# A float32 product split into high and low parts: other engines write the parts of its first instance, and its last chunk goes tile by tile

## The reference

```python
# x: 8 x 1024 x 512, cond: 8 x 512; D = 512
ae = layernorm(cond, ln_g, ln_b)
h = gelu(ae @ w1 + b1)                       # exact gelu
x_a, x_b = split(h @ w2 + b2)                # each 8 x 512 x 8 (rank 8)
layer = base_layer + einsum('bdr,bkr->bdk', x_a, x_b)
x = x + (x + einsum('btc,bco->bto', x, layer))          # first layer
ys = cond / sqrt(D)
d = rsqrt(einsum('bi,io->bo', ys*ys, weight*weight) + 1e-8)
x = x + einsum('bsi,io->bso', x * ys[:, None, :], weight) * d[:, None, :]
```

## Time and profile before

| what | value |
| --- | --- |
| median of 3 runs | 293.89 us (293.83 to 294.56) |
| profiled execution: its own time, and its span | 293.79 us, 292.1 us |
| PE busy | 287.6 us (98%) |
| PEld busy | 226.5 us (78%) |
| DVE busy | 198.8 us (68%) |
| ACT busy | 153.5 us (53%) |
| POOL busy | 18.1 us (6%) |
| mean granted TensorE clock | 0.998 of full speed |

### The profile page before, as it was taken

The page is one execution under the profiler, slowest core; times in us unless marked ns, Lnnn a source line. Parts: engine busy times, 40 slices in busy tenths (PEclk is TensorE's granted clock), DMA queues, the critical chain, the costliest instruction groups (busy, mean ns, idle before and its releaser), DMA issues.

```text
span 292.1 us, 3792 instructions
## 1 busy us (share of the span) xinstructions
PE 287.6 (98%) x1400; PEld 226.5 (78%) x1400; DVE 198.8 (68%) x309; ACT 153.5 (53%) x233; POOL 18.1 (6%) x35
## 2 busy tenths in 40 slices
PE   8999999999999999999999999999999999999995
PEld 8775566657688888888888888888888888888884
DVE  4889342237577899994699988766783749762672
ACT  4763141306373548774548765634781645443951
POOL 5000000000131202000202000020000000000000
PEclk9999999999999999999999999999999999999999
DMA  6998899987042311589512589201132493101205
GB/s 189 368 426 300 324 406 384 362 311 281 2 120 89 153 72 72 166 263 378 203 72 109 181 266 417 109 0 72 72 139 79 147 362 142 72 0 74 106 38 215
DMA packets 13409, 55.05 MB, mean 188 GB/s; under 512 B 1616, under 2 KB 1616, under 8 KB 11088
## 3 DMA queue, kind: packets, MB, share of 16 engines
q1 hardware_dynamic: 10368, 44.07, 41.1%
q10 hardware_dynamic: 3024, 10.75, 9.3%
HBM read 38.03 MB, written 16.78 MB: 188 GB/s over the span
## 4 chain that ended last, share of the span: by engine, by line
PE 97%; DVE 1%; issue 0%; ACT 0%; POOL 0%; ACTq 0%; POOLq 0%
PE tile L1143 30%; PE tile L1174 26%; PE tile L992 12%; PE aux L1028 6%; PE acc L960 5%; PE tile L1109 4%; PE tile L975 3%; PE spare L1028 3%; PE acc L1028 3%; PE tile L931 2%; PE aux L1014 1%; PE aux L938 1%; PE aux L1082 1%; PE spare L1014 1%; PE acc L1014 1%; DVE rs L664 0%
## 5 line engine op out<-in xcount | busy, mean ns | idle before, releaser
L1143 PE MATMUL tile<-xs,qs 128*128 128x512 f32 x384 | 90.3, 389 | 0.0
L1143 PEld LDWEIGHTS tile<-xs,qs 128*128 128x128 f32 x384 | 72.1, 188 | 15.0
L1174 PE MATMUL tile<-xs,qs 128*128 128x512 f32 x336 | 77.5, 389 | 0.0
L1174 PEld LDWEIGHTS tile<-xs,qs 128*128 128x128 f32 x336 | 63.1, 188 | 13.1
L767 DVE TENSOR_TENSOR xs<-stream,xs 128x1024 fp32r<-128x1024 f32 x30 | 36.2, 1219 | 12.6 <-ACT xs L428 12.4
L483 ACT ACTIVATE stream<-tile,dts 128x512 f32<-128x512 f32 x32 | 21.8, 688 | 36.4 <-PE tile L1143 36.4
L372 ACT CAST rs<-rtmp 128x512 fp32r<-128x512 f32 x32 | 19.9, 621 | 37.2 <-PE tile L992 24.2
L664 DVE TENSOR_TENSOR rs<-rtmp,rs 128x512 fp32r<-128x512 f32 x32 | 22.0, 688 | 25.6 <-ACT rs L372 25.2
L992 PE MATMUL tile<-rs,w0s 128*128 128x512 f32 x144 | 34.7, 395 | 0.1
L992 PEld LDWEIGHTS tile<-rs,w0s 128*128 128x128 f32 x144 | 26.5, 188 | 10.0 <-issue 4.2
L428 ACT CAST xs<-stream 128x1024 fp32r<-128x1024 f32 x30 | 31.1, 1048 | 3.7 <-ACT stream L483 2.3
(11 more groups left out here) (139 smaller groups left out, 247.7 us busy)
## 6 DMA issues: line engine op xcount, KB each, us to landing
stream<-in_w2u SPq DMA_DIRECT2D x13, 1024.0 KB, 8.7
stream<-in_xT SPq DMA_DIRECT2D x20, 512.0 KB, 5.9
out<-stream ACTq DMA_DIRECT2D x20, 512.0 KB, 2.6
xr<-in_xT SPq DMA_DIRECT2D x12, 512.0 KB, 5.0
out<-stream SPq DMA_DIRECT2D x11, 512.0 KB, 3.0
xr<-in_w2u SPq DMA_DIRECT2D x3, 1024.0 KB, 7.7
w1s<-in_w1n SPq DMA_DIRECT2D x4, 256.0 KB, 5.1
base<-in_wm SPq DMA_DIRECT2D x1, 1024.0 KB, 8.1
```

The source lines that it names most:

```text
L1143: last = nc.tensor.matmul(tiles[o][:], q_slot(b, cc)[:, u, cols], x_slot(b, (h, cc // 2))[:, v, cc % 2], start=cc == 0 and (u, v) == (0, 0 ...
L1174: last = nc.tensor.matmul(tiles[bank + m][:], q_slot(b, q)[:, u, cols], x_slot(b, x)[:, v, k], start=opens and k == 0 and (u, v) == (0, 0) ...
```

## The change

- DVE writes the high part of chunks 0 and 1 of R_0 itself: `r_direct` is the scaling pass with its output in `rs` (fp32r). The pass into `rtmp` is still made, a little later, since the low part needs it. ACT's two casts r_high(0, 0) and r_high(0, 1) go.
- POOL adds the 2s: it builds a matrix `ident2` with 2 on the diagonal (a memset and an affine_select, before the other constants), and adds it to each of the four diagonal blocks as they land. DVE's four add_two go. These four adds stand ahead of the sixteen casts for perm.
- The last chunk of the first product goes tile by tile, three matmuls for each tile, and starts once both low parts are there. The transposition for the hidden layer follows tile 1.
- The small steps of the layernorm come later in DVE's list, behind both parts of chunk 1. In the norms' chain w0_low(3) moves behind the first step, and r_low(0, 3) behind the last.
- On ACT the cast w0_high(1) moves ahead of w1_square(1).

```diff
+            nc.gpsimd.memset(ident2, 2.0).then_inc(pool_step, 1)
+            pool.wait_ge(pool_step, 5)
...
+            nc.gpsimd.affine_select(out=ident2, in_=ident2, compare_op=ALU.is_equal, fill=0.0, base=0,
+                                    pattern=[[-1, P]], channel_multiplier=1).then_inc(twos_ready, 1)
...
+            pool.wait_ge(twos_ready, 1)
+            for kc in range(KC):
+                pool.wait_ge(w0_loaded[kc], 16)
+                blk = w0raw[:, kc, kc * P:(kc + 1) * P]
+                nc.gpsimd.tensor_tensor(blk, ident2, blk, ALU.add).then_inc(w0_eyed, 1)
...
             w0_high(0)
-            r_high(0, 0)
             w1_square(0)
...
+            w0_high(1)
             w1_square(1)
-            w0_high(1)
-            r_high(0, 1)
...
+            def r_direct(kc):
+
+                nc.vector.tensor_scalar(rs[:, kc, 0], w1s[:, kc], ys[:, ORDER[0], kc:kc + 1], None,
+                                        ALU.mult).then_inc(r_hi, 1)
...
-            add_two(0)
             dve.wait_ge(w1_loaded[0], 16)
-            r_scale(0, 0)
+            r_direct(0)
             dve.wait_ge(sum_done, 3)
             step(nc.vector.tensor_scalar(row(2, B), aux[0][:, 64:64 + B], 1.0 / D, LN_EPS, ALU.mult, ALU.add))
             w0_low(0)
+            r_scale(0, 0)
             r_low(0, 0)
-            add_two(1)
             dve.wait_ge(w1_loaded[1], 16)
+            r_direct(1)
+            w0_low(1)
             r_scale(0, 1)
+            r_low(0, 1)
...
+                kc = KC - 1
+                pe.wait_ge(w0_lo, KC)
+                pe.wait_ge(r_lo, KC)
+                for cc in range(KC):
+                    for u, v in ((0, 0), (0, 1), (1, 0)):
+                        last = nc.tensor.matmul(tiles[cc][:], w0s[:, u, kc, cc * P:(cc + 1) * P], rs[:, kc, v],
+                                                start=False, stop=(u, v) == (1, 0))
+                    last.then_inc(tile_done, 1)
+                    if cc == 1:
+                        between(kc, 1, 0)
```

More of the change, by code:

```diff
@@ L91, in cond_residual_kernel @@
         w0nat = base[:, 4]
+        ident2 = base[:, 0, 0, 0:P]
         asp, csp = qs[:, 4, 0], qs[:, 4, 1]
@@ L121, in cond_residual_kernel @@
         mask_ready = sem("mask_ready")
+        twos_ready = sem("twos_ready")
+        first_scaled = sem("first_scaled")
         ys_ready = sem("ys_ready")
@@ L327, in _ @@
             nc.gpsimd.memset(eye4[:], 0.0).then_inc(pool_step, 1)
-            pool.wait_ge(pool_step, 4)
+            nc.gpsimd.memset(ident2, 2.0).then_inc(pool_step, 1)
+            pool.wait_ge(pool_step, 5)
             nc.gpsimd.affine_select(out=ident[:], in_=ones[:], compare_op=ALU.is_equal, fill=0.0, base=0,
                                     pattern=[[-1, P]], channel_multiplier=1).then_inc(consts_ready, 1)
+            nc.gpsimd.affine_select(out=ident2, in_=ident2, compare_op=ALU.is_equal, fill=0.0, base=0,
+                                    pattern=[[-1, P]], channel_multiplier=1).then_inc(twos_ready, 1)
             nc.gpsimd.affine_select(out=sel3, in_=sel3, compare_op=ALU.not_equal, fill=1.0, base=0,
@@ L369, in r_high @@
             def r_high(b, kc):
-                act.wait_ge(r_eyed, b * KC + kc + 1)
+                act.wait_ge(r_eyed, b * KC + kc - 1)
                 rs_free(act, b, kc)
@@ L635, in _ @@
                                     mybir.AxisListType.X, ALU.add).then_inc(sum_done, 1)
[L637 to L640, removed]
             def w0_low(kc):
@@ L653, in r_scale @@
                 if b == 0:
-                    scaled.then_inc(r_eyed, 1)
+                    scaled.then_inc(r_eyed if kc > 1 else first_scaled, 1)
                     return
@@ L660, in r_scale @@
                                                ALU.add).then_inc(r_eyed, 1)
+            def r_direct(kc):
+                nc.vector.tensor_scalar(rs[:, kc, 0], w1s[:, kc], ys[:, ORDER[0], kc:kc + 1], None,
+                                        ALU.mult).then_inc(r_hi, 1)
             def r_low(b, kc):
                 dve.wait_ge(r_hi, b * KC + kc + 1)
+                if b * KC + kc < 2:
+                    dve.wait_ge(first_scaled, kc + 1)
                 nc.vector.tensor_tensor(rs[:, kc, 1], rtmp[:, kc % RTMP], rs[:, kc, 0].bitcast(F32),
@@ L675, in r_build @@
                 r_low(b, 3)
-            dve.wait_ge(consts_ready, 1)
-            add_two(0)
             dve.wait_ge(w1_loaded[0], 16)
-            r_scale(0, 0)
+            r_direct(0)
             dve.wait_ge(sum_done, 3)
@@ L692, in _ @@
             step(nc.vector.scalar_tensor_tensor(row(0, B), row(7, B), 1.5, row(5, B), ALU.add, ALU.mult))
-            w0_low(1)
-            r_low(0, 1)
-            add_two(2)
             dve.wait_ge(w1_loaded[2], 16)
@@ L703, in _ @@
             r_low(0, 2)
-            add_two(3)
             dve.wait_ge(w1_loaded[3], 16)
             r_scale(0, 3)
-            w0_low(3)
-            r_low(0, 3)
             dve.wait_ge(d2_turned, 1)
             d_next(nc.vector.tensor_scalar(by_chunk(3), turned(1), D_EPS, None, ALU.add))
+            w0_low(3)
             dve.wait_ge(d_root, 1)
@@ L718, in _ @@
                                            dts[:].rearrange("p b k -> p k b"), by_chunk(3), ALU.mult))
+            r_low(0, 3)
             r_scale(1, 0)
@@ L964, in first_base @@
             def first_base(between):
-                for kc in range(KC):
+                for kc in range(KC - 1):
                     for u, v in ((0, 0), (1, 0), (0, 1)):
@@ L975, in first_base @@
                             last = nc.tensor.matmul(tiles[cc][:], w0s[:, u, kc, cc * P:(cc + 1) * P], rs[:, kc, v],
[L976 to L980, removed]
+                                                    start=kc == 0 and (u, v) == (0, 0), stop=False)
+                        if v:
                             last.then_inc(r_used, 1)
                         between(kc, u, v)
+                kc = KC - 1
[8 more added lines that the diff above has]
+                        between(kc, 1, 0)
             def base_tiles(b, between):
```

## The result

The changed kernel takes 295.06 us (median of 11 executions, 294.53 to 295.58), and the kernel before 293.89 us in as many beside it. The ratio is 1.0033, with a 95% interval from 1.0023 to 1.0044. That is 0.3% slower, and 0.4 us above the upper end of the forecast range (293.3 to 294.7).

The account below looks back on a forecast made before the run. PE was taken to bound the kernel (97% of the chain that ended last), with 0.50 us of gaps here. 293.79 - 0.05 + 0.1 = 293.84, the median 0.10 above that execution: forecast 293.9 us, range 293.3 to 294.7.

Parts of the forecast that it names:

- DVE then starts w0_low(2) no later than before: Ahead of chunk 2: the net 0.38 us of added DVE work fits into 0.61 of idle time.
- the path in my working: From chunk 2's 2s through the norms' copy, chain, z and Gelu to the evacuation of tile 2: -0.05 us in sum.
- the first of the two gaps: In chunk 2 PE waits for ACT's copy of the norms before their transposition: 0.14 us lost, to be gained.
- no slack left: At chunk 3: r_low(0, 3) is done at 17.87, PE arrives at 17.86 and starts 0.13 us earlier than before.
- the gap at tile 2: In the second product's first chunk: PE waits 0.44 us for tile 2's bank, so nearly nothing is won.
- rival 3: POOL's add slow or locked out by DVE passes, or a slow fp32r pass: 294.1 to 295.0 us, chance 0.20.
- in each other's way only beside the casts, with 0.1: Around chunk 2: POOL's sixteen casts stretch three DVE passes by 0.28 us at most, entered as 0.1.
- The high parts by DVE: Chunks 0 and 1: PE has no gap there, so the first matmul stays at 6.96 and nothing is gained.
- the gap of 0.36: Ahead of the second product PE waits for tile 0's evacuation; going tile by tile would gain 0.36 us here.
- the fp32r output: DVE's direct scaling pass was taken at 0.48 us, as with float32 output, with bounds 0.48 and 0.68.
- rival 1: Both PE gaps close and nothing takes their place: 0.50 us gained, 293.4 us, chance 0.12.

Follow-up runs that it names:

- e6: Kernel before with only DVE's direct high parts, the moved layernorm steps and cast w0_high(1): ratio 1.0029 to before, span 293.30 us.
- e4: Kernel before with only the last chunk of the first product tile by tile: ratio 0.9996 to before, span 292.06 us.
- e1: Kernel before run again with no edit: ratio 1.0007 to before, span 292.39 us.
- e11: Kernel before with only GpSimd's building of the matrix of 2s, no add: ratio 1.0002 to before, span 292.37 us.
- e14: Kernel before with six small GpSimd memsets behind its casts: ratio 1.0020 to before, 2.12 us outside the span.
- e8: Kernel before with one unread two-input GpSimd add behind its casts: ratio 1.0002 to before, 1.74 us outside the span.
- e10: Kernel before with only GpSimd's four waits on W0's loads ahead of its casts: ratio 1.0018 to before, span 292.63 us.
- e13: Kernel before with four small unread GpSimd adds behind its casts: ratio 1.0005 to before, 1.76 us outside the span.
- e9: Changed kernel run again with no edit: ratio 1.0032 to before, span 292.87 us.
- e3: Changed kernel with the adds of the 2s given back to DVE: ratio 1.0033 to before, span 293.19 us.
- e7: Changed kernel with w0_low(3) and r_low(0, 3) put back ahead of the norms' chain: ratio 1.0012 to before, span 292.50 us.
- e5: Changed kernel with the high parts of chunks 0 and 1 given back to ACT's casts: ratio 1.0014 to before, span 292.54 us.
- e2: Kernel before with only GpSimd writing and adding the 2s, DVE's four adds gone: ratio 1.0009 to before, span 292.25 us.
- e15: Kernel before with GpSimd's adds of the 2s behind its sixteen casts: ratio 1.0007 to before, span 292.32 us.
- e12: Kernel before with the last chunk tile by tile and three warm-ups less: ratio 0.9987 to before, span 291.82 us.
- e16: Second sample of the kernel with the last chunk tile by tile and three warm-ups less: ratio 0.9979 to before, span 291.81 us.

## Why the prediction was wrong

**Where it failed first: DVE's balance ahead of chunk 2.** The step that failed is "DVE then starts w0_low(2) no later than before", with the landing of W0's chunk 2 setting the pace. It started at 12.60 instead of 12.03, and the pace was set by DVE's own list. I set two passes of 0.48 less two adds of 0.29, which is 0.38, against an idle time of 0.61. From the step that reads the sum to the scaling of chunk 2, DVE took 5.45 us (6.13 to 11.58). Before, its list up to the third add took 4.04 (6.11 to 10.15, where 10.15 is the last start, 9.55, and the 0.60 from one such pass to the next). What is new sums up like this: two r_scale with their own waits (0.58 each) and a direct pass (0.40) in place of one r_scale (0.39) and one add (0.21) are 0.96, and two passes stretched beside GpSimd's adds (0.81 for 0.69, 0.43 for 0.17) are 0.38. That is 1.3 of the measured 1.4, and I had 0.4. Of the 1.4, the time up to 10.85 in which DVE had waited takes up 0.70, and the third add, which no longer stands there, 0.21. About 0.5 is left: the scaling of chunk 2 starts at 11.58 instead of 11.06. I had counted durations and not the list: of the two adds that go, one stood in idle time anyway, two passes have a wait that was not there before, and the idle time shrinks when the list starts late. e6 shows the size with DVE's adds kept: this part alone costs 1.0 us of span.

**What it did downstream.** The 0.61 went through the copy of the norms, the chain, z and the evacuation of tile 2, as the path in my working says, and came out as the w2 matmuls 0.43 later where I had them 0.05 earlier, which is 0.48 of the 0.61. The path was right, its entry was not. On this path PE waits in three places, not in one. In e4's trace, where it waits nowhere, it is 4.08 us from the start of chunk 2 to that of chunk 3 (13.87 to 17.95), and 3.04 from the second product to the w2 matmuls. In the changed kernel these are 4.61 (13.94 to 18.55) and 3.28 (21.31 to 24.59). So 0.53 go ahead of chunk 3, to the late transposition and the late r_low, and 0.24 at tile 2. Measured like this, the first of the two gaps in the kernel before is larger than I read it: its chunk 2 takes 4.35 (13.65 to 18.00), so 0.27 are lost there and not 0.14. And it is a gap of some executions only. In the traces of e1, e11 and e14 the transposition isn't waited for.

**The execution to execution scatter, taken as fixed.** I worked from one trace, in which the second small sum loads at 5.29. In others it loads at 5.13 to 6.13, with ten warm-up loads ahead of it that take 1.20 to 2.25 us; the granted clock reads full in all of them. With the lists of before, a sum at 5.71 (e1) gives w2 matmuls at 24.21 and one at 6.13 (e11) gives 24.80. All of this comes from PE itself, whose first product starts that much later (7.28 and 7.86): from there to the w2 matmuls it is 16.93 and 16.94, and over the seven traces in which DVE's list is that of before (before, e1, e8, e10, e11, e13, e14) 16.93 to 17.35, on average 17.08.

In the changed kernel it is 17.33 and, in e9, 17.94, on average 0.55 more. Here DVE's list has the last word, and w2 follows the step that reads the sum. From the first trace to e9 that step is 0.53 later (6.13 and 6.66) and w2 1.14 later (24.59 and 25.73). The other 0.6 is the longer way to r_scale(0, 3), 8.33 for 7.73, with the late chunk 1 in it. e3, without GpSimd's adds and with DVE's, has 17.92, so it doesn't take a late GpSimd add to get there. A mean span 0.64 longer fits these traces, and 0.4 in the first pair was one draw. That is argued from two traces of the changed kernel, and no run shows how often a chunk lands late.

**The norms' chain.** I had it with no slack left, and expected no loss by it, since the evacuation of tile 2 would come out where it was. That order was itself a cost: e7, with the chain put back, closes the gap at tile 2 and takes 0.46 off the span. The two losses (0.42 by e5, 0.46 by e7) come to more than the whole 0.64, since both end in the same evacuation. Both parts taken back together were not run.

**POOL.** The add takes 0.45 with DVE idle beside it (e5, at 5.02; forecast 0.50), and up to 0.89 (e2) and 1.00 (e15) beside DVE passes (rival 3, in part). The add of chunk 2, on which rival 3 turned, took 0.64 in the changed kernel's trace (the longest of its four), and DVE didn't wait for it. By the Trainium skill ("GPSIMD Engine Reference", section 3.1) my estimate had been 0.56 (0.57 when multiplied out); the measurement is 0.45. The mutual lock of "SBUF — State Buffer", section "Who interferes with whom", of the Trainium skill fits what was seen on both engines: where the add at 7.33 kept its 0.46, the DVE pass at 7.52 took 0.81 instead of 0.69, and in e2 an add at 6.70 took 0.89. My sum had the two engines in each other's way only beside the casts, with 0.1. There w0_low(2) took 0.73 instead of 0.69 (12.60), and r_low(2) and r_scale(0, 3) what they always take, so 0.04 would have done.

**Outside the span.** 0.28 us of the loss were in no step and in no rival: the sum put this term at nothing without a reason. I had taken the 1.7 us outside as a constant. The runs show 1.74 for the list of before and 2.02 for that of the change, and the trace, which ends with the span, doesn't contain the difference.

**What was right.** The high parts by DVE start nothing earlier; the last chunk by tiles closes the gap of 0.36 (e4 against e1, 16.57 for 16.93); no gap is left ahead of the second product; the gap at tile 2 (0.44 forecast, 0.38 measured); the fp32r output costs nothing (0.48). That e12 and e16 come out where rival 1 had the changed kernel, 0.5 us under before, is a coincidence: 0.36 of it is the gap by tiles, and they also have three warm-ups less, which rival 1 doesn't have.

**What stays open.** Why the length of GpSimd's list has a step in the time outside between four and six added instructions, and whether it lies ahead of the span or behind it. Why the warm-up loads run at half pace for a varying time (ten in the two microseconds from 4 in e9, nineteen in e10). What the moved layernorm steps cost by themselves. And the 0.3 us of e10.

## What to carry to other kernels

Before work is moved to an engine that "has idle time", write down its list between two fixed events, with each pass's start-to-start time and its new waits, and see whether the idle time is still there when the list starts late; an idle stretch that waits for a transfer is also what absorbs scatter. Test the parts of a bundle one by one: here one part was worth about 0.1%, which is inside the noise of twelve runs and visible only in the traces, and the others cost more. And look at the time outside the span too, since a few instructions on an idle engine can cost more there than they would save inside.

## What was new about the hardware

- Six more instructions on GpSimd add 0.25 to 0.38 us to the mean time outside the span (1.99 to 2.12 against 1.74), and no execution with them is under 1.95; four more add nothing (1.76).
- A two-input add of GpSimd over 128x128 float32 takes 0.45 us alone (e5), and up to 0.89 (e2) and 1.00 (e15) beside DVE passes; a DVE pass over 128x8 took 0.43 instead of 0.17 beside it. GpSimd's sixteen casts took 2.49 us early on, and 3.9 to 4.8 beside DVE's low passes (e9 and e7).
- A tensor_scalar of DVE with fp32r output takes 0.48 us for 128x512, as with float32 output.
- The same ten warm-up loads took from 1.20 to 2.25 us from one execution to the next, while the granted clock read 1.00 in that stretch (from 4 to 6 us) and 0.998 to 1.0 over the whole execution.
